# A decoder layer as one software-pipelined program: a straight stream of due times in place of a loop of ticks

## The chip, the cores and the metric

The kernel runs on one core of one Trainium2 chip. The metric is device time in microseconds, the median of several executions. Before the change it is 1157.1 us (three runs, 1156.52 to 1158.71). Line numbers (L896) are those of the kernel before.

## The reference, cut to what matters

Two sequences of 1024 tokens, 256 wide, go through three blocks in fp32, each followed by a residual and a layer norm:

```
x = LN(x + mamba(x))          # rmsnorm, in_proj to 2*512, causal conv of 4 taps, silu, x_proj to (16+16+16),
                              # delta = softplus(dt_proj), scan s = s*exp(delta*A) + delta*B*u over 16 states,
                              # y = sum_n C_n s_n + D*u, y * silu(z), out_proj, + x
x = LN(x + cross_attn(x))     # 8 heads of 32, rope on queries and keys, two sets of 64 keys with one softmax,
                              # out_proj, + x, LN, one expert's linear layer, relu
x = LN(x + moe(x))            # 8 gated experts of 256 and a shared one, top 2 of 8 by softmax, all computed densely
```

Only expert 3 of the cross attention is used. All nine experts of the last block are computed for every token, the weights being zero for those not chosen.

## The kernel before, in words

The 2048 tokens are four chunks of 512 (NT = 4 tiles of 128 rows). Chunks 0 and 1 are one sequence, 2 and 3 the other. The work on a chunk has a *mixer* part (first block) and a *second* part (attention and experts), and the program overlaps the scan of chunk i with the second part of chunk i-1.

One written-out order, SCHEDULE, is walked by each of the five engines (SP issues DMAs); each engine picks the steps in which it has work, and its queue runs them strictly in that order. Semaphores order the engines among each other. `streams` runs the order once for chunk 0 alone, three times in a hardware loop (Fori), and once for the last chunk's second part alone ("drain").

A pass begins with the *pre* steps of chunk i and the last *post* steps of chunk i-1, no scan running: transposes of x, the input projection (L857), convolution (L1140), Silu, the x projection (L829), transposes to C (ctok), the rank product (L836), softplus, delta * u = v on DVE, and for the chunk before the output product (L851), residual and first norm. Then come 35 ticks. In a tick DVE does two scan units (L1105; a unit is one state and 128 channels, 512 steps) and sums two finished state tiles into yacc (L1155); ACT makes the two decays exp(delta*A) in PSUM (L674); POOL multiplies v by the broadcast row of B (L563); PE transposes state tiles (L778). Between these steps, "early", "mid", "half" and "late" carry the second part of the previous chunk by its own tick number.

In the second part, tiles of the attention take two ticks each: score (L896), maximum (L1257), soft maximum on ACT (L729, L733), transpose (L945), copy (L740), value product (L952), scale, small transpose, copy, output projection (L960, L961), sum and statistics. The rope of the queries is made by an ACT copy, a DMA that swaps neighbouring rows, two POOL multiplies and two POOL additions (L583, L587). Then norm, feed-forward (L977, L978), relu, norm, transposes split in a high and a low part, gate logits, top two, weights. The experts are 18 half steps c (nine experts, two halves): first product a (L928), Identity and Tanh on ACT (L766, L768), weighing by the router on POOL (L596), gate product on DVE (L1196), second input product b (L928), hidden product on DVE (L1266) and the second expert product w2 (L908), which adds into two PSUM banks. One half step is done per tick. In PE's queue the order is a(c), w2(c-1), b(c), with the state transposes between.

The two decay buffers are PSUM banks 0 and 1, the state transposes use 2 and 3, the second part 4 to 7; in the drain the first banks serve the experts too. All DMAs are issued from SP's queue in order.

Of the kernel before, what the change touches and what calls it, by code (L numbers as in the profile page):

```python
# [41 lines left out]
HRING = 3  # L43
PREP = 2
DRING = 3
EPS = 1e-5
LINEAR = 30.0
# [13 lines left out]
T_X1T, T_Q, T_ROT, T_S, T_PT = 0, 1, 2, 3, 4  # L61
T_RES = T_PT + 2 * (NT - 1) + 4
T_LNT, T_FFN, T_X2, T_X2T, T_GATE, T_TOP = range(T_RES + 1, T_RES + 7)
T_EXP = T_TOP
T_OUT = T_EXP + 2 * ALL + 1
PRE_TICKS = 2
SCAN_TICKS = 2 * NS + 3


def schedule():  # L70

    tick = lambda t: [("early", t), ("mid", t), ("half", t), ("late", t)]
    steps = [("setup", 0), ("pre", 1), ("post", 3), ("post", 4), ("pre", 2), ("post", 5), ("pre", 3)] + tick(0)
    steps += [("pre", 4), ("pre", 5), ("early", 1), ("pre", 6), ("late", 1), ("setup", 1)]
    for t in range(2, PRE_TICKS):
        steps += tick(t)
    for s in range(SCAN_TICKS):  # L80
        t = PRE_TICKS + s
        steps += [("early", t), ("sum", s), ("mid", t), ("scan", s), ("half", t), ("scan2", s), ("late", t)]
        if 2 <= s < 2 + 2 * ALL + PREP:
            steps.append(("prep", s - 2))
        if SCAN_TICKS - 12 <= s < SCAN_TICKS - 8:
            steps.append(("fetch", s - SCAN_TICKS + 12))
    steps.append(("prep", 2 * ALL + PREP))
    for k, t in enumerate(range(PRE_TICKS + SCAN_TICKS, T_OUT + 1)):
        steps += [("post", k)] if k < 3 else []
        steps += tick(t)  # L90
    return steps


SCHEDULE = schedule()


class Signal:
# [7 lines left out]
    def at(self, j, k):  # L105
        return self.sem, j * self.per + k + 1


def bank_a(c, drain):

    return 0 if drain and c % 2 else 4


def bank_b(c, drain):

    return 1 if drain and c % 2 else 5


def is_first(j):

    return isinstance(j, int) and j == 0


def block_kernel(nc, x, w_in, w_out, w_xp, w_dt, w_q, w_k, w_ks, w_v, w_o, w_f, w_gate, w13, w2, b2, vecs, rows,
                 ctx_t, rope_q, rope_k, out):
    ctx = ExitStack()
    with ctx:
# [15 lines left out]
        wdt = sb("wdt", [RANK, DI])  # L143
# [5 lines left out]
        b2s = sb("b2s", [ALL, DM])  # L149
        vec = sb("vec", [P, VECS])  # L150
        row = sb("row", [1, 2, DM])
        kblk = sb("kblk", [P, SEQS, HB * 2 * KEYS])
        vx = sb("vx", [P, SEQS, HEADS * (HD + 1)])
        ident = sb("ident", [P, P])
        ones = sb("ones", [1, P])
        iota_i = sb("iota_i", [P, EXPERTS], I32)
        iota8 = sb("iota8", [P, EXPERTS])
        keep = sb("keep", [P, CHUNKS])
        power = sb("power", [P, NT])
        neg_a = sb("neg_a", [P, Q * NS])  # L160
# [4 lines left out]
        xt = sb("xt", [P, NT, DM])  # L165
        xn = sb("xn", [P, NT, DM])
        u = sb("u", [P, Q, TC])
        sz = sb("sz", [P, Q, TC])
        delta = sb("delta", [P, Q, TC])
# [3 lines left out]
        hs = sb("hs", [P, 2, Q, TC + 4])  # L173
# [3 lines left out]
        ctok = sb("ctok", [P, NT, NS])  # L177
# [6 lines left out]
        xi = hs[:, 1, :, :]  # L184
        xnt = yacc[:, NT // 2:NT, :]


        x1 = sb("x1", [P, NT, DM])
        x1t = sb("x1t", [P, KD, TC])
        work = sb("work", [P, 4096 + 1024])  # L190
        qr = work[:, 0:2048].rearrange("p (b t) -> p b t", b=HB)
        qs = work[:, 2048:4096].rearrange("p (b t) -> p b t", b=HB)
        qc = [work[:, 4096:5120].rearrange("p (b t) -> p b t", b=2), x1t]
        prob = work[:, 3072:4096]
        probt = work[:, 4096:5120]
        ga = work[:, 1024:2048].rearrange("p (a t) -> p a t", a=2)
        gac = work[:, 2048:3072].rearrange("p (a t) -> p a t", a=2)
        gm = work[:, 3072:4096].rearrange("p (a t) -> p a t", a=2)
        hh = work[:, 4096:5120].rearrange("p (a t) -> p a t", a=2)
# [4 lines left out]
        on = sb("on", [P, DM])  # L204
        ont = sb("ont", [P, KD, P])
# [1193 lines left out]
```

## Time and profile before

| what | value |
|---|---|
| median of three runs | 1157.1 us |
| the profiled execution, whole | 1156.59 us |
| its span, first to last instruction | 1154.8 us |
| mean granted TensorE clock | 0.825 of full |
| busy in the span: PE, DVE, ACT, POOL | 898.6, 793.7, 501.0, 469.3 us |
| first to last scan of chunk 0 | 62.6 to 177.2 us |

The page gives the busy time by engine, a strip in 40 slices, the DMA queues and the chain of work that ended last. The chain is the view to read for this kernel: it goes back from the last instruction to what released it, and so shows which engine's work is in the way and where. Idle time of an engine that is not in the chain costs nothing by itself. The rows used are in the section below.

### The profile page before, as it was taken

Reading aid. Unit: us, or ns where it says so; the run is one execution under the profiler, and the core shown is the slowest. Engines: PE = TensorE matmul, PEld = TensorE weight load, DVE = VectorE, ACT = ScalarE, POOL = GpSimd, SP = SyncE. Lnnn points to the kernel's source line nnn. Section 1 sums busy time; section 2 is a strip of 40 time slices with the busy share of each in tenths; the row PEclk is TensorE's granted clock in tenths of the full one; section 3 lists DMA queues with packets and bytes.
Section 4 is the critical chain, followed back from the end, with each engine's and each line's share of the span. In section 5 each row is a group of like instructions: output and inputs, shape, how many; then the busy total and the mean of one; then the engine's idle time right before and its main releaser. Section 6 shows DMA issues by size and latency. Waiting matters only on the chain.

```text
span 1154.8 us, 13667 instructions
## 1 busy us (share of the span) xinstructions
PE 898.6 (78%) x3960; PEld 681.7 (59%) x3960; DVE 793.7 (69%) x1239; ACT 501.0 (43%) x957; POOL 469.3 (41%) x281
## 2 busy tenths in 40 slices
PE   4934558947879998857789999577799975867995
PEld 2433446446658885356568875265588862645884
DVE  1699996568898957569989864599989751213333
ACT  3545451745434624645535516465445322312232
POOL 1259970074445731273627510654537413000222
PEclk9955557869679999779789999697789996756998
DMA  6136611110205431102025411112045412001451
GB/s 205 47 103 237 234 37 26 67 37 26 103 28 178 152 110 57 74 22 107 19 74 184 154 56 67 64 37 92 19 147 167 153 37 109 1 0 37 155 182 55
DMA packets 43439, 105.65 MB, mean 91 GB/s; under 512 B 4447, under 2 KB 13288, under 8 KB 43358
## 3 DMA queue, kind: packets, MB, share of 16 engines
q1 hardware_dynamic: 43358, 104.68, 26.6%
q8 instruction: 37, 0.61, 0.2%
q14 instruction: 44, 0.36, 0.1%
HBM read 88.73 MB, written 11.74 MB: 87 GB/s over the span
## 4 chain that ended last, share of the span: by engine, by line
PE 61%; DVE 12%; issue 10%; POOL 9%; ACT 5%; DVEq 0%; POOLq 0%; ACTq 0%
PE ps L928 17%; PE ps L908 11%; PE ps L778 9%; PE ps L857 5%; PE ps L896 4%; POOL dbu L563 4%; DVE hs L1105 4%; PE ps L851 2%; PE ps L952 2%; POOL parts L551 2%; PE ps L977 2%; PE ps L836 2%; POOL work L583 2%; DVE yacc L1155 1%; PE ps L960 1%
## 5 line engine op out<-in xcount | busy, mean ns | idle before, releaser
L563 POOL TENSOR_TENSOR dbu<-v,bbc 128x1024 f32<-128x1024 f32 x128 | 301.8, 2368 | 202.5 <-DVE v L1090 117.6
L1105 DVE TENSOR_TENSOR_SCAN hs<-ps,carry,dbu 128x512 f32<-128x512 f32 x256 | 317.1, 1269 | 2.6 <-issue 1.4
L674 ACT ACTIVATE ps<-delta,neg_a 128x512 f32<-128x512 f32 x256 | 176.2, 692 | 231.7 <-DVE hs L1105 231.5
L778 PE MATMUL ps<-ident,hs 128*128 128x128 f32 x1024 | 183.3, 337 | 98.4 <-DVE yacc L1155 83.5
L778 PEld LDWEIGHTS ps<-ident,hs 128*128 128x128 f32 x1024 | 154.8, 177 | 126.6 <-DVE hs L1105 76.8
L928 PE MATMUL ps<-x_hi,parts 128*128 128x512 f32 x576 | 181.4, 438 | 0.0
L596 POOL TENSOR_TENSOR work<-work,cbc 128x512 f32<-128x512 f32 x64 | 82.1, 1283 | 228.4 <-ACT work L766 228.4
L1155 DVE SCALAR_TENSOR_TENSOR yacc<-ps,ctok,yacc 128x512 f32<-128x512 f32 x240 | 167.3, 738 | 1.2 <-PE ps L778 1.0
L908 PE MATMUL ps<-w2s,work 128*128 128x256 f32 x576 | 136.8, 380 | 3.6 <-DVE work L1266 3.6
L908 PEld LDWEIGHTS ps<-w2s,work 128*128 128x128 f32 x576 | 108.2, 189 | 23.1 <-DVE work L1266 5.3
L928 PEld LDWEIGHTS ps<-x_hi,parts 128*128 128x128 f32 x576 | 109.7, 199 | 19.0 <-DVE work L1196 0.6
L766 ACT ACTIVATE work<-ps,half_b 128x512 f32<-128x512 f32 x72 | 49.5, 687 | 153.4 <-PE ps L928 153.4
L1196 DVE SCALAR_TENSOR_TENSOR work<-ps,work 128x512 f32<-128x512 f32 x72 | 49.7, 691 | 88.2 <-POOL work L596 82.1
L896 PE MATMUL ps<-kblk,work 128*128 (+1 forms) x128 | 47.6, 537 | 61.2 <-POOL work L587 47.4
L928 PE MATMUL ps<-x_lo,parts 128*128 128x512 f32 x288 | 92.6, 403 | 0.0
L896 PEld LDWEIGHTS ps<-kblk,work 128*128 128x128 f32 x128 | 33.6, 275 | 72.6 <-issue 55.8
L1266 DVE SCALAR_TENSOR_TENSOR work<-ps,vec,work 128x512 f32<-128x512 f32 x72 | 53.2, 739 | 27.4 <-PE ps L928 21.0
L928 PEld LDWEIGHTS ps<-x_lo,parts 128*128 128x128 f32 x288 | 56.1, 195 | 13.4
L1257 DVE TENSOR_REDUCE mx<-ps 128x8 f32<-128x1024 f32 x16 | 19.5, 1217 | 62.8 <-PE ps L896 62.8
L857 PE MATMUL ps<-yacc,win 128*128 128x512 f32 x128 | 58.3, 616 | 0.8 <-ACT yacc L630 0.8
L768 ACT ACTIVATE ps<-ps,half_b 128x512 f32<-128x512 f32 x72 | 47.0, 653 | 0.0
L569 POOL TENSOR_TENSOR rstd_x<-ve_x,power 128x4 f32<-128x4 f32 x8 | 8.1, 1008 | 93.3 <-DVE ve_x L1176 93.3
(165 smaller groups left out, 1093.6 us busy)
## 6 DMA issues: line engine op xcount, KB each, us to landing
parts<-parts_dram SPq DMA_DIRECT2D x72, 512.0 KB, 3.6
bbc<-brow_dram SPq DMA_DIRECT2D x32, 512.0 KB, 4.5
parts_dram<-parts SPq DMA_DIRECT2D x18, 512.0 KB, 4.0
w2s<-in_w SPq DMA_DIRECT2D x36, 256.0 KB, 4.0
cbc<-comb_dram SPq DMA_DIRECT2D x32, 256.0 KB, 3.6
w13s<-in_w SPq DMA_DIRECT2D x18, 256.0 KB, 3.1
work<-work SPq DMA_DIRECT2D x16, 256.0 KB, 2.3
xn<-in_x SPq DMA_DIRECT2D x5, 512.0 KB, 5.3
```

The lines of the kernel that those rows point to most:

```text
L563: pool.tensor_tensor(dbu[:, i % DRING, :, :], v[:, 2 * h:2 * h + 2, :], bbc[:, n // 2 % 2, n % 2, :].rearrange("p (o t) -> p o t", o=1) .t ...
L596: pool.tensor_tensor(gac[:, ib, :], ga[:, ib, :], cbc[:, g % CRING, :], ALU.mult).then_inc(gac_done.sem, 1)
L674: act.activation(ps[:, unit % 2, :], delta[:, q, :], ACT.Exp, scale=neg_a[:, q * NS + m:q * NS + m + 1]).then_inc(da_done.sem, 1)
L778: last = pe.transpose(ps[:, bank, t * P:(t + 1) * P], src(t), ident[:, :])
L857: last = pe.matmul(ps[:, m % Q, :], win[:, k, m * P:(m + 1) * P], xnt[:, k, :], start=(k == 0), stop=(k == KD - 1))
L896: last = pe.matmul(ps[:, 4 + b // 2, b % 2 * 2 * KEYS:(b % 2 + 1) * 2 * KEYS], qr[:, b, tile * P:(tile + 1) * P], kblk[:, bass.ds(j // CPS ...
L908: last = pe.matmul(out_cols(tile), hh[:, ib, tile * P:(tile + 1) * P], w2s[:, e % WRING, ib * DM:(ib + 1) * DM], start=False, stop=(c == 2 ...
L928: last = pe.matmul(o, left(l, k).bitcast(F32R), right(r, k).bitcast(F32R), start=(i == 0 and k == 0), stop=(i == len(terms) - 1 and k == K ...
L1105: dve.tensor_tensor_scan(hs[:, m % 2, q, 0:TC], ps[:, unit % 2, :], dbu[:, n % DRING, q % 2, :], carry[:, m, q:q + 1], ALU.mult, ALU.add). ...
L1155: dve.scalar_tensor_tensor(out=yacc[:, t, :], in0=ps[:, 2 + t % 2, :], scalar=c, in1=yacc[:, t, :], op0=ALU.mult, op1=ALU.add).then_inc(y_ ...
L1196: dve.scalar_tensor_tensor(out=gm[:, ib, :], in0=ps[:, bank_a(c, drain), :], scalar=1.0, in1=(gac if c >= 2 else ga)[:, ib, :], op0=ALU.ad ...
L1266: dve.scalar_tensor_tensor(out=hh[:, ib, :], in0=ps[:, bank_b(c, drain), :], scalar=col("b3", c), in1=gm[:, ib, :], op0=ALU.add, op1=ALU.m ...
```

## The change

The loop, SCHEDULE and the tick numbers go. Instead there are tables of due times within a period of 32 ticks, sorted by time; `period(j)` merges three chunks: the scan of chunk j, the second part of j-1 (BEFORE, TILE, EXPERT) and the pre steps of j+1 (AHEAD). All five passes are written out. There is no pre stage between scans: the projection, convolution and softplus of the next chunk are among the ticks of the present one. In a tick, PE's state transposes are due at 0.37, and scan units 2n and 2n+1 follow each other on DVE, as do the two decays on ACT, at 0.4. Attention tiles are one tick apart, experts 0.95; steps whose due time is past 32 stand after the last scan of their period. For the last chunk's second part (the fifth period) there is no scan.

```diff
+OWN = {"gates_in_0": 2.7, "gates_raw_0": 3.2, "gates_in_1": 4.5, "gates_raw_1": 5.0, "gates_silu": 14.7}
+BEFORE = {
+    "y_turn": 2.05, "y_skip_1": 2.65, "y_skip_0": 2.95, "y_gate_0": 3.45, "y_gate_1": 3.65,
+    "out_0": 3.7, "out_1": 4.1, "residual_0": 4.35, "residual_1": 4.66, "stats_x1": 4.95, "rstd_x1": 5.05,
+    "norm_x1": 5.4, "x1_turn": 5.7, "x1_keep": 5.9, "query_0": 6.1, "query_1": 6.3, "rope_0": 6.65, "rope_1": 6.95,
+    "stats_xl": 12.65, "rstd_xl": 12.66, "norm_xl": 12.7, "xl_turn": 12.8, "xl_keep": 12.9,
+    "ffn": 13.0, "relu_0": 13.45, "relu_1": 13.65, "stats_x2": 13.7, "rstd_x2": 13.8, "norm_x2": 14.0,
+    "x2_turn": 14.2, "x2_high": 14.4, "x2_low": 14.65, "w2_load": 14.66, "logits": 14.8, "top_two": 15.3, "score_exp": 15.35,
+    "combine": 15.65, "comb_turn": 15.7, "comb_keep": 15.8, "comb_store": 15.82, "out_bias": 16.8,
+    "experts_load": 12.5, "rope_load": 1.7, "x1_load": 0.5,
+}
+TILE = {"score": 7.2, "maximum": 7.65, "soft": 7.7, "p_turn": 8.0, "p_keep": 8.1, "over": 8.15, "over_scale": 8.65,
+        "o_turn": 8.72, "o_keep": 8.76, "o_proj": 9.17, "attended": 9.6}
+TILE_STEP = 1.0
+GATE0, GATE_STEP = 15.8, 0.95
+EXPERT = {"a": 0.0, "gate": 0.01, "w2": 0.1, "b": 0.12, "weigh": 0.13, "product": 0.6, "hidden": 0.95}
+AHEAD = {
+    "x_load": 0.0, "squares": 1.5, "mean_sq": 1.9, "rms": 1.95, "x_scale": 3.0, "x_turn": 5.3, "x_keep": 5.6,
+    "edge": 10.0, "in_0": 11.8, "in_keep_0": 12.3, "conv_0": 12.95, "in_1": 13.4, "in_keep_1": 13.6, "conv_1": 14.1,
+    "edge_keep": 14.12, "conv_silu": 14.71, "xproj": 15.0, "rows_keep": 15.1, "rows_store": 15.11, "c_turn": 15.2,
+    "c_keep": 15.34, "dt_0": 15.4, "soft_in_0": 15.45, "dt_1": 15.75, "soft_in_1": 15.85, "dt_2": 16.1,
+    "soft_in_2": 16.15, "dt_3": 16.3, "soft_in_3": 16.35, "soft_exp": 16.7, "soft_ln": 16.9, "delta": 17.3,
+    "v_0": 28.5, "v_1": 29.5,
+}
+SETUP = {"setup_load": 0.01, "setup_zero": 0.02, "setup_work": 8.5, "setup_keys": 9.5}
...
+        found += [(s + at, name, s, j) for s in range(TICKS) for at, name in ((0.0, "sum"), (0.38, "rows"), (0.4, "scan"))]
...
+        for c in range(2 * ALL + 1):
+            for name, at in EXPERT.items():
+                k = c - 1 if name == "w2" else c
+                if 0 <= k < 2 * ALL:
+                    found.append((GATE0 + GATE_STEP * c + at, name, k, j - 1))
...
+    return [step[1:] for step in sorted(found, key=lambda step: step[0])]
```

Other edits that the steps below touch. The scores sum two products, of the queries times cosine with the keys and of the queries times swapped sine with keys whose neighbouring rows are swapped; the swap is made once per sequence by DMA, and the rope of the queries is two DVE passes per block:

```diff
+                    for b in range(HB):
+                        for s, side in enumerate((qc, qs)):
+                            last = pe.matmul(ps[:, 4 + b // 2, b % 2 * 2 * KEYS:(b % 2 + 1) * 2 * KEYS],
+                                             side[:, b, n * P:(n + 1) * P], kblk[:, s, b * 2 * KEYS:(b + 1) * 2 * KEYS],
+                                             start=(s == 0), stop=(s == 1))
```

Softplus is written as Relu(p) + Ln(1 + Exp(-|p|)), with Abs and Relu on ACT for each of the four channel blocks, Exp and Ln on two blocks at a time, and the sum on POOL; v = delta * u goes from DVE to POOL. The gate half z is copied out raw and put through Silu later, next to the convolution's Silu:

```diff
+                if name == "gates_silu":
+                    act.wait_ge(*zraw_done.at(j, Q))
+                    for h in range(2):
+                        z = sz[:, 2 * h:2 * h + 2, :]
+                        act.activation(z, z, ACT.Silu).then_inc(sz_done.sem, 1)
+                if name == "conv_silu":
+                    for h in range(2):
+                        act.wait_ge(*conv_done.at(j, (TAPS - 1) * 2 * (h + 1)))
+                        c = us[j % 2][:, 2 * h:2 * h + 2, :]
+                        act.activation(c, c, ACT.Silu).then_inc(u_done.sem, 1)
+                    act.preload_act_table(ACT.Exp)
...
+                if name == "delta":
+                    for h in range(2):
+                        pool.wait_ge(*above_done.at(j, Q))
+                        pool.wait_ge(*ln_done.at(j, h + 1))
+                        d = deltas[j % 2][:, 2 * h:2 * h + 2, :]
+                        pool.tensor_tensor(d, above[:, 2 * h:2 * h + 2, :], d, ALU.add).then_inc(delta_done.sem, 1)
```

u, delta and ctok are double; x1 is loaded with x and the residual is made in place; x2 shares its tile with xa; some weight rings share a tile with the convolution's input. The key and value setup on PE and DVE moves from before the first scan to tick 8.5 of the first period.

## Rows read from the trace of the kernel before

**Rows 1.** The page's first part: busy us, share, instructions by engine.
```profile
PE 898.6 (78%) x3960; PEld 681.7 (59%) x3960; DVE 793.7 (69%) x1239; ACT 501.0 (43%) x957; POOL 469.3 (41%) x281
```
**Rows 2.** The chain of waits in order of time, whole span: start, us, what.
```profile
242.85 3.67 PE ps L896 x8
...
497.75 3.79 PE ps L896 x8
...
619.18 1.73 PE ps L908 x8
624.55 1.73 PE ps L908 x8
...
689.66 1.86 issue
...
746.33 3.79 PE ps L896 x8
...
974.01 3.80 PE ps L896 x8
```
**Rows 3.** The chain of waits from 555 to 600 us.
```profile
555.61 1.98 ACT xa L685 x4
...
588.34 0.20 DVE comb L1318
```
**Rows 4.** Timeline of PE, 450 to 522 us: start, us, line, operation, tiles, count.
```profile
450.49 13.90 PE L857 MATMUL ps<-yacc,win 128*128 128x512 f32 x32
...
513.72 1.09 PE L945 MATMUL ps<-ident,work 128*128 128x128 f32 x8 [0.28 <-ACT work L733]
514.65 0.38 PE L778 MATMUL ps<-ident,on 128*128 128x128 f32 x2
516.88 1.97 PE L896 MATMUL ps<-kblk,work 128*128 x8 [1.85 <-ACT ont L745]
...
519.56 1.03 PE L960 MATMUL ps<-wo,ont 128*128 128x256 f32 x4
520.52 0.69 PE L961 MATMUL ps<-row,ones 1*128 1x256 f32 x2
521.14 1.97 PE L952 MATMUL ps<-vx,work 128*128 x16
```
**Rows 5.** The page's fifth part, costliest groups: busy and mean ns, idle before.
```profile
L563 POOL TENSOR_TENSOR dbu<-v,bbc 128x1024 f32<-128x1024 f32 x128 | 301.8, 2368 | 202.5 <-DVE v L1090 117.6
```
**Rows 6.** Timeline of DVE, 53 to 619 us.
```profile
53.66 2.15 DVE L1029 SCALAR_TENSOR_TENSOR work<-ps,vec,work 128x128 f32<-128x128 f32 x8
...
455.50 7.38 DVE L1140 SCALAR_TENSOR_TENSOR u<-hs,vec,u 128x512 f32<-128x512 f32 x11 [0.96 <-ACT u L692]
...
519.20 1.20 DVE L1257 TENSOR_REDUCE mx<-ps 128x8 f32<-128x1024 f32 x1
...
615.93 0.69 DVE L1196 SCALAR_TENSOR_TENSOR work<-ps,work 128x512 f32<-128x512 f32 x1 [0.26 <-POOL work L596]
616.53 1.27 DVE L1105 TENSOR_TENSOR_SCAN hs<-ps,carry,dbu 128x512 f32<-128x512 f32 x1
617.73 0.72 DVE L1266 SCALAR_TENSOR_TENSOR work<-ps,vec,work 128x512 f32<-128x512 f32 x1
```
**Rows 7.** The DMA issues: size and median us from issue to landing.
```profile
xn<-in_x SPq DMA_DIRECT2D x5, 512.0 KB, 5.3
```
**Rows 8.** Timeline of ACT, 477 to 523 us.
```profile
477.30 1.28 ACT L667 ACT_TABLE_LOAD   x1
478.59 2.19 ACT L667 ACTIVATE delta<-delta 128x512 f32<-128x512 f32 x4
...
516.64 1.01 ACT L740 ACTIVATE work<-ps 128x1024 f32<-128x1024 f32 x1
...
520.68 2.18 ACT L733 ACTIVATE work<-ps,top 128x128 f32<-128x128 f32 x8
```
**Rows 9.** Instructions on tile hs, 60 to 182 us: duration min/median/max ns, first and last start.
```profile
L1105 DVE TENSOR_TENSOR_SCAN hs<-ps,carry,dbu x64: 1256/1259/1283, 62.6 to 177.2; 128x512 f32<-128x512 f32 x64
```

More of the change, by code:

```diff
@@ L57 @@
 VECS = _at
[L61 to L91, printed above, removed]
@@ L369, in block_kernel, with streams, bank_a, bank_b @@
         block = ctx.enter_context(nc.Block())
-        def streams(eng, mixer, second):
-            def body(i, first, last):
-                for kind, step in SCHEDULE:
-                    if kind in ("early", "mid", "half", "late"):
-                        if not first:
-                            second(i - 1, step, kind, last)
-                    elif kind == "post" and step >= 3:
-                        if not first:
-                            mixer(i - 1, kind, step)
-                    elif kind in ("setup", "prep"):
-                        if first:
-                            mixer(i, kind, step)
-                    elif kind == "fetch" and not last:
-                        mixer(i + 1, kind, step)
-                    elif not last:
-                        mixer(i, kind, step)
-            for step in range(4):
-                mixer(0, "fetch", step)
-            body(0, True, False)
-            with eng.Fori(1, CHUNKS, 1) as i:
-                body(i, False, False)
-            body(CHUNKS, False, True)
+        def streams(step):
+            for name, at in sorted(AHEAD.items(), key=lambda item: item[1]):
+                step(0, *numbered(name), False)
+            for j in range(CHUNKS + 1):
+                for name, n, chunk in period(j):
+                    step(chunk, name, n, j == CHUNKS)
+        def bank_a(c, drain):
+            return 0 if drain and c % 2 else 4
+        def bank_b(c, drain):
+            return 1 if drain and c % 2 else 5
+        def out_cols(tile):
+            return ps[:, 6 + tile // 2, tile % 2 * DM:(tile % 2 + 1) * DM]
         @block.sync
@@ L848, in mixer @@
+                if name == "out":
+                    for t in (2 * n, 2 * n + 1):
                         for q in range(Q):
@@ new lines, in step @@
+                if name == "over":
+                    pe.wait_ge(*pt_done.at(j, n + 1))
+                    for h in range(HEADS):
+                        c = slice(h * (HD + 1), (h + 1) * (HD + 1))
+                        last = pe.matmul(ps[:, 6, c], probt[:, h * P:(h + 1) * P], vx[:, j // CPS, c],
+                                         start=True, stop=True)
+                    last.then_inc(av_ps.sem, 1)
+                if name == "o_turn":
+                    pe.wait_ge(*on_done.at(j, n + 1))
+                    pe.wait_ge(*p_done.at(j, min(n + 2, NT)))
+                    transposes(5, lambda k: on[:, k * P:(k + 1) * P], KD, ont_ps)
```

1336 lines of the change are left out of this document (666 added, 670 removed).

## The prediction

> **What bounds the kernel now.** I read the busy line first: PE is busy 898.6 us of 1154.8 and DVE 793.7 [rows 1]; neither is full, so the end is set by waits. The chain of waits in order of time says which. The first score product of each of the four chunks' second layers starts at 242.85, 497.75, 746.33 and 974.01 [rows 2], so a chunk costs 254.9, 248.6 and 227.7 us, and from the last of these marks to the end are 180.8. The chain runs through the second layer of the previous chunk (scores, soft maximum, feed-forward, experts); the scan of the current chunk only rides along.
>
> I cut the 248.6 us between the second and third mark into four pieces. (a) Score to the start of the attention's layer norm at 555.61 [rows 3]: 57.9. (b) To the end of the routing weights at 588.54 [rows 3]: 32.9. (c) To the end of the last second expert product at 689.66 [rows 2]: 101.1. In (c) the same expert product recurs at 619.18 and 624.55 [rows 2], every 5.37 us. (d) To the next first score: 56.7, with the skip, gates, output product, both input projections, softplus and rope in it. The test of the change is whether these four pieces shrink.
>
> **The change, part by part.** (1) The loop becomes a straight stream, and the projection, convolution and softplus of the chunk ahead (formerly in d, 45 us with the scan standing still) go between the scan ticks. That frees much of d: half of the input projection (32 issues take 13.90 [rows 4], so a half is 6.9), the x projection (8 issues, 3.5), the rank product (8 issues, 3.5) and the wait for softplus leave it, and the rope no longer goes through a DMA swap and four POOL passes of about the 2.37 us of a POOL multiply over 128x1024 [rows 5]. But the old d began under the last experts; the new one begins only after the final sum. I walk it. Final sums and statistics 3.4. Three pairs of old sums (1.3 each) with two pairs of new scans between (2.4 each [rows 6]): 8.7. DVE's mean of squares stands in this queue and waits for ACT's squares, which come behind its decays (2.4) and behind a load that is queued after the previous output's store and lands in 5.3 [rows 7]: 2 to 6, I take 4. From y's transposes (16 at the pace of 8 in 1.09 [rows 4]) through skip, gate projection, a scan pair and the gate 12. Output product 7. From there through the second half of the gate projection, decays and statistics to the norm 9, transposes and copy 2.7, query product 6.9 (16 issues at the projection's pace), last rope pair 1.4. Together 55.1: (d) is 1.6 shorter.
>
> On the loop's edge PE shows 1.86 us of issue at 689.66 [rows 2], which the straight stream drops; the walk has no such item, so it is already credited. The Trainium skill (Runtime: NRT & Kernel Launch, section "Instruction fetch mechanics") says that a taken branch breaks the sequential prefetch and is a reason to unroll. The row allows at most that for each of three edges, 6 us; a longer stall than this is not in the trace.
>
> (2) Attention: one tile per scan tick instead of one per two, and each score now sums two products (query by keys, swapped query by swapped keys) in place of one. In PE's new order score n+1 stands behind transpose, value product and output projection of the tiles before. So a tile is a ring with no slack: small transpose 0.4, transpose 1.05, copy 1.05, value product 1.95, output projection with its bias row 1.7, score twice 1.8, that is 3.65, maximum 1.2, soft maximum with its bias 2.5: 13.5 us (PE's parts from [rows 4], ACT's from [rows 8], the maximum from [rows 6]). Beside it DVE has one tick (3.7) and 2.7 of tile work, so nothing fills its wait. Piece (a): first score and soft maximum 7.4, three rings 40.5, the last tile 14 (its chain of 4.5, output projection of the tile before 1.7, a state transpose 1, the half input projection that now stands in PE's queue 3.5, its own projection 1.7, residual and copies 1.6), norm statistics 2: 63.9, 6 more than before.
>
> (3) Piece (b): both halves of the convolution (6 taps of 0.67 [rows 6], 4 each) and a Silu block are in it. The block is two table loads of 1.28 [rows 8] and four wide activations of about 1.05 (the 128x1024 copy took 1.01 [rows 8]): 6.8 on ACT. The copy of the x projection is queued behind it, the transpose to C behind that, and DVE's C copy, which stands before the scan and the routing weights, waits for all of them. Norm and copies 4.5, feed-forward 6.7 (four output projections), relu, norm and transposes 10, the second convolution half and a scan 3.5 before the copy to high parts, logits and selection 6, then the wait and the scan 6, weights 2.6: 39.3, 6.4 more.
>
> (4) Piece (c): the Abs and Relu of softplus (8 at 0.65, 5.2), Exp 2.1, Ln and two loads 4.7 are ACT instructions ahead of the third gate, and POOL has the two delta additions (2.37 each [rows 5]) ahead of the third expert's weighing. Three expert steps so take about 21 instead of 16. The other 15: PE needs 5.37 a tick before and after. With the two scans as one block, the hidden product leaves DVE 3.0 after the gate product (two scans of 1.2, 0.65 [rows 6]), when PE has been through a state transpose (1) and the next first half (1.3): PE waits 0.7 in some steps and recovers it in others; I take 5.45, bounds 5.3 and 6.0. The last two steps run after the scan has ended, so they are 2 shorter. (c) is 106.4, 5.3 more. That the second product is one tick nearer in the tables leaves PE's sequence (first half, previous second product, second half) as it was: 0.
>
> The four pieces give 264.7, so a steady chunk is 16 slower. The first gap has no store ahead of the load, 2 less: 262.7, 8 above its 254.9. The third has no chunk ahead: without the half projections, both convolutions, Silu and softplus and with a shorter (d), 231, 3 slower.
>
> (5) Before the first mark. The setup on DVE (53.66 until the first scan at 62.6 [rows 6, 9], 8.9) moves behind the first scans, and half the input projection leaves the start; against it POOL now does two additions, two multiplies and a first product in a row (11.8 [rows 5]) before the second tick. I set the first scan at 58. The 64 scans spread over 62.6 to 177.2 [rows 9], 116 us with the last; into these come the convolution 8, setup 9, and waits: the squares 2.5, PE's setup 3, Silu block and x projection about 9 and softplus about 6, of which some cover each other: I take 15, bounds 0 and 25. That puts the end of this scan at 206 and the first mark at 257, 14 later.
>
> (6) After the last mark: three rings at 13.5 in place of 10 (the score at 516.88 and the value product at 521.14 show the full clock; at 974.01 a score took 3.80 instead of 1.97, the low level [rows 2, 4]); bounds 0 and +30, I take +14, since PE has more to do per ring and its clock rose in the drain's loop before.
>
> Sum against the profiled execution: 1154.8 + 14 + 8 + 16 + 3 + 14 = 1209.8, and 1.8 around the span (1156.59 for that execution, within 0.05% of the median 1157.1): **1212**.
>
> The Trainium skill (ScalarE: Activation LUTs, section "What ACT_TABLE_LOAD costs") gives a load about 1.28 us and a drain of 1.38 after it. The trace shows the load, and the next activation 0.01 us after it (477.30 and 478.59) [rows 8]; by the page the two blocks, four loads, would add 5.5 a period and the sum would be about 1228. I follow the row.
>
> **Rivals.** *Full overlap (0.14).* If the waits in (a) to (c) are covered because the engines run far ahead, a chunk costs what DVE has to do: 793.7 / 4 = 198 [rows 1], with the serial tail 215. First mark as before, 242.9 + 215 + 215 + 195 + 181 + 2 = 1051. For it: DVE idles in both pre stages today. Against: the ring in (2) has one owner of each step, and a queue in order can't pass it. It decides at a ring of about 10 us or less. *ACT blocks hidden (0.14).* The ring is as I say, but decays and gates slip past Silu and softplus: 11 less in two chunks, 5 in the third, 15 at the start, so 1170; the copies before them leave some slack. *All offsets (0.06).* The four pieces and the start end as long as they were: 1157. *Low clock in the rings (0.05).* PE waits in each ring, and its parts (8.75) nearly double: 7.6 more in 9 rings, 1280. The 3.80 us score speaks for it, the 1.97 against.
>
> **Numbers.** The forecast, 1180 to 1245 by itself, has 0.61. The range 1148 to 1255 takes in the hidden blocks and the even case, and leaves out full overlap and the low clock, 0.19. About 0.2% is what this measurement can tell from no change. Faster: 0.14 and a third of the even case, 0.16; same 0.03; slower 0.81.
>
> **What would show it.** Right: successive scores 13 to 14 us apart in the attention stage, DVE idle there on PE; DVE's C copy waiting on ACT after a Silu block; the third gate product late, behind softplus; expert steps of 5.4 to 5.5. The first score of the second layer at about 257, 520, 785. Wrong: score spacing at 10 or less, or scan ticks that go on at 5 us through the attention; then the period is near 215 and the kernel is much faster.

## The result, and the profile after

The changed kernel takes 1388.95 us (median of 4 runs, 1383.93 to 1391.93), 1.200 times the kernel before (95% interval 1.196 to 1.204; 1156.81 in the same job). I had forecast 1212, slower by 55, and a range that ended at 1255. The direction was right; the loss is 232 us, four times what I gave it.

The page's first and second part for the kernel after, which answer to [rows 1] (busy us, share, instructions; then the granted TensorE clock in 40 slices, 9 being nine tenths of full speed or more):

```profile
PE 1031.0 (74%) x4088; PEld 754.9 (54%) x4088; DVE 782.2 (56%) x1202; ACT 507.6 (37%) x915; POOL 476.5 (34%) x275
...
PEclk9577655776667999876668999876569998655898
```

The clock line of the kernel before, for comparison:

```profile
PEclk9955557869679999779789999697789996756998
```

PE's busy time grew by 132 us for 3% more instructions, while the other engines moved by under 12. The doubled scores are some 29 us of that (16 tiles at 1.83, the forecast's price at the full level); for the rest, the same kind of product takes longer. The clock line tells why. Its mean is 0.775 against 0.825 before, and the 5s and 6s come back once in each chunk.

The chain of waits of the kernel after, in order of time (start, us, what), the four marks that answer to [rows 2]:

```profile
293.97 3.73 PE ps L929 x16
...
604.51 3.73 PE ps L929 x16
...
911.68 3.73 PE ps L929 x16
...
1176.00 3.73 PE ps L929 x16
```

The span ends at 1388.0. By these marks the time went as follows; the last column is the run with three remedies together, told below (times of the profiled execution).

| stretch | before | forecast | after | e12_sum |
|---|---|---|---|---|
| to the first score | 242.9 | 257 | 294.0 | 281.2 |
| first to second | 254.9 | 262.7 | 310.5 | 276.5 |
| second to third | 248.6 | 264.7 | 307.2 | 275.8 |
| third to fourth | 227.7 | 231 | 264.3 | 231.3 |
| fourth to the end | 180.8 | 194 | 212.0 | 183.4 |

Here is one attention tile of the kernel after (timeline of PE, ACT and DVE, a selection; in brackets how long the engine stood idle before, and what ended that):

```profile
611.99 1.39 PE L939 MATMUL ps<-ident,work 128*128 128x128 f32 x8 [2.89 <-ACT work L740]
...
614.50 3.62 PE L946 MATMUL ps<-vx,work 128*128 128x33 f32 x16 [1.11 <-ACT work L747]
...
617.93 6.14 PE L929 MATMUL ps<-kblk,work 128*128 128x256 f32 x16
...
624.11 1.23 DVE L1202 TENSOR_REDUCE mx<-ps 128x8 f32<-128x1024 f32 x1 [5.28 <-PE ps L929]
...
625.61 2.18 ACT L740 ACTIVATE work<-ps,top 128x128 f32<-128x128 f32 x8
...
627.93 0.41 PE L794 MATMUL ps<-ident,rows_t 128*128 128x128 f32 x2 [2.98 <-ACT work L740]
...
637.00 0.42 DVE L1224 TENSOR_TENSOR xa<-ps,x 128x256 f32<-128x256 f32 x1 [7.98 <-PE ps L959]
```

The reader is to see two things. The ring is the one that I had walked: score, maximum, soft maximum, transpose, value product, and DVE idle on PE in each link. But the value product takes 3.62 where [rows 4] had 1.97, and the score 6.14 where the first one of a chunk takes 3.72. The same stretch in four windows of one microsecond (the window, its length, PE's busy us and count, granted clock, DMA share, GB/s):

```profile
611.00:612.00 1.00, 0.01 (x1) 1.00 0.00 0
613.00:614.00 1.00, 0.39 (x2) 0.50 0.00 0
621.00:622.00 1.00, 1.00 (x4) 0.50 0.00 0
624.00:625.00 1.00, 0.94 (x9) 1.00 0.00 0
```

PE stands idle for 2.9 us on the soft maximum, works less than 1 us at the full level, and then the granted clock is 0.50 (1.2 GHz) until about 622.7; it comes back for the end of the score and the state transposes, and the next wait begins. So from the second score of a chunk on, scores stand 18.3 to 20.1 us apart where I had 13.5; from the first to the second, where no output projection stands between, 13.4 to 14.0.

Two more places. The first convolution half of the next chunk now runs between scan ticks, beside POOL's products (DVE's timeline for chunks 1 and 2, counted from 0, and the combine weights; then POOL's timeline at the same times):

```profile
128.54 9.20 DVE L1053 SCALAR_TENSOR_TENSOR u<-shared,vec,u 128x512 f32<-128x512 f32 x5 [0.30 <-ACT u L651]
...
375.18 6.15 DVE L1053 SCALAR_TENSOR_TENSOR u<-shared,vec,u 128x512 f32<-128x512 f32 x6
...
426.80 2.14 DVE L1311 TENSOR_TENSOR pr<-el,re 128x32 f32<-128x32 f32 x1
```

```profile
127.66 1.71 POOL L567 TENSOR_TENSOR parts<-xa,parts 128x512 fp32r<-128x512 f32 x1
129.33 2.79 POOL L543 TENSOR_TENSOR dbu<-v,bbc 128x1024 f32<-128x1024 f32 x1
...
426.55 2.35 POOL L543 TENSOR_TENSOR dbu<-v,bbc 128x1024 f32<-128x1024 f32 x1 [14.11 <-DVE hs L1164]
```

A tap takes 1.84 us there (five in 9.20) where [rows 6] had eleven in 7.38, 0.67 each. POOL's product takes 2.79 instead of 2.35 beside them, and a product of 32 columns takes 2.14 and ends when POOL's does. Both taps' operands are in SBUF; the sums and scans, with one operand in PSUM, keep their 0.70 and 1.23 beside the same POOL products.

And the expert step after, with its scan block (ACT, POOL and DVE):

```profile
480.09 0.69 ACT L614 ACTIVATE ps<-delta,neg_a 128x512 f32<-128x512 f32 x1 [0.48 <-DVE hs L1164]
...
480.72 0.67 ACT L782 ACTIVATE work<-ps,half_b 128x512 f32<-128x512 f32 x1
...
481.47 1.27 POOL L595 TENSOR_TENSOR work<-work,shared 128x512 f32<-128x512 f32 x1 [2.21 <-ACT work L782]
...
482.84 0.69 DVE L1258 SCALAR_TENSOR_TENSOR work<-ps,work 128x512 f32<-128x512 f32 x1 [0.82 <-issue]
...
483.44 2.45 DVE L1164 TENSOR_TENSOR_SCAN hs<-ps,carry,dbu 128x512 f32<-128x512 f32 x2
...
485.93 0.69 ACT L614 ACTIVATE ps<-delta,neg_a 128x512 f32<-128x512 f32 x1 [0.48 <-DVE hs L1164]
...
486.56 0.67 ACT L782 ACTIVATE work<-ps,half_b 128x512 f32<-128x512 f32 x1
```

This is a ring that my walk of (c) did not have: gate product, both scans, the decay behind the second scan, and only then on ACT the next gate, its weighing on POOL, and the next product, 5.84 us after the last. [rows 2] have 5.37. Later in the stage, where the drift of 0.05 tick a step has put the sums ahead of the hidden product, steps are 6.0.

### The profile page after: what moved, and what is told of

It reads as the page before. It is cut to its first block, busy times and chain, and to the rows that moved or that the text cites. A ratio compares the mean times of both kernels' runs of the same rounds, so it can differ in the third digit from the quotient of the medians.

```text
span 1388.0 us, 12836 instructions
## 1 busy us (share of the span) xinstructions
PE 1031.0 (74%) x4088; PEld 754.9 (54%) x4088; DVE 782.2 (56%) x1202; ACT 507.6 (37%) x915; POOL 476.5 (34%) x275
## 4 chain that ended last, share of the span: by engine, by line
PE 43%; issue 16%; DVE 13%; POOL 13%; ACT 9%; DMA 1%; DVEq 0%; POOLq 0%; ACTq 0%; SPq 0%
POOL dbu L543 9%; PE ps L929 6%; PE ps L808 6%; DVE hs L1164 4%; PE ps L946 4%; PE ps L1013 4%; PE ps L794 4%; PE ps L917 3%; PE ps L974 2%; ACT work L740 2%; PE ps L799 2%; PE ps L958 2%; DVE yacc L1148 2%; POOL work L595 2%; PE ps L939 1%
## 5 line engine op out<-in xcount | busy, mean ns | idle before, releaser
L543 POOL TENSOR_TENSOR dbu<-v,bbc 128x1024 f32<-128x1024 f32 x128 | 309.4, 2419 | 276.5 <-DVE hs L1164 275.5
L1164 DVE TENSOR_TENSOR_SCAN hs<-ps,nothing,dbu 128x512 f32<-128x512 f32 x128 | 156.7, 1266 | 31.1 <-POOL dbu L543 27.0
L1164 DVE TENSOR_TENSOR_SCAN hs<-ps,carry,dbu 128x512 f32<-128x512 f32 x128 | 156.7, 1266 | 0.0
L1013 PE MATMUL ps<-shared,work 128*128 128x256 f32 x576 | 143.3, 393 | 15.4 <-DVE work L1266 14.7
L595 POOL TENSOR_TENSOR work<-work,shared 128x512 f32<-128x512 f32 x64 | 81.6, 1275 | 185.4 <-ACT work L782 185.4
L1013 PEld LDWEIGHTS ps<-shared,work 128*128 128x128 f32 x576 | 107.7, 193 | 46.4 <-DVE work L1266 16.6
L808 PEld LDWEIGHTS ps<-x_hi,parts 128*128 128x128 f32 x576 | 110.1, 198 | 30.6 <-issue 10.8
L929 PE MATMUL ps<-kblk,work 128*128 128x256 f32 x256 | 85.4, 506 | 3.4 <-DVE work L1196 3.4
L929 PEld LDWEIGHTS ps<-kblk,work 128*128 128x128 f32 x256 | 66.1, 265 | 23.3 <-issue 5.2
L799 PE MATMUL ps<-xnt,win 128*128 128x512 f32 x128 | 72.0, 717 | 1.9 <-ACT rows_t L752 1.1
L946 PE MATMUL ps<-vx,work 128*128 128x33 f32 x256 | 58.0, 403 | 17.8 <-ACT work L747 17.8
L946 PEld LDWEIGHTS ps<-vx,work 128*128 128x128 f32 x256 | 55.8, 330 | 23.2 <-ACT work L747 23.2
L808 PEld LDWEIGHTS ps<-x_lo,parts 128*128 128x128 f32 x288 | 56.0, 195 | 13.5
```

Source lines behind the costliest of these rows:

```text
L543: pool.tensor_tensor(dbu[:, (j * TICKS + i) % DRING, :, :], v[:, 2 * h:2 * h + 2, :], bbc[:, n // 2 % 2, n % 2, :].rearrange("p (o t) -> p ...
L595: pool.tensor_tensor(gac[:, ib, :], ga[:, ib, :], cbc[:, g % CRING, :], ALU.mult).then_inc(gac_done.sem, 1)
L799: last = pe.matmul(ps[:, bank, :], win[:, k, m * P:(m + 1) * P], xnt[:, k, :], start=(k == 0), stop=(k == KD - 1))
L808: last = pe.matmul(ps[:, bank, :], parts[:, c % HRING, part, (s * KD + k) * P:(s * KD + k + 1) * P].bitcast(F32R), right[:, k, :].bitcast( ...
L929: last = pe.matmul(ps[:, 4 + b // 2, b % 2 * 2 * KEYS:(b % 2 + 1) * 2 * KEYS], side[:, b, n * P:(n + 1) * P], kblk[:, s, b * 2 * KEYS:(b + ...
L946: last = pe.matmul(ps[:, 6, c], probt[:, h * P:(h + 1) * P], vx[:, j // CPS, c], start=True, stop=True)
```

## The experiments

All edits are to the changed kernel. Medians are of 4 runs; the ratios are to the kernel before, which ran on the same chip (1154.65, 1155.40 and 1155.49 in the three jobs). The changed kernel's own ratio is 1.200 (1.196 to 1.204). "Less" in us is against its 1388.95, which comes from the job where the kernel before took 1156.81; differences of 2 us between jobs mean nothing.

**e1_warm: keep PE busy in the tile.** Idle transposes are products whose result nobody reads.

```diff
+WARM_TURN, WARM_OVER = 24, 9
...
 if name == "p_turn":
+    pe.wait_ge(*on_done.at(j, n))
+    for _ in range(WARM_TURN):
+        pe.transpose(ps[:, 6, 0:P], ident[:, :], ident[:, :])
     pe.wait_ge(*p_done.at(j, n + 1))
-    pe.wait_ge(*on_done.at(j, n))
...
 if name == "over":
+    for _ in range(WARM_OVER):
+        pe.transpose(ps[:, 4, 0:P], ident[:, :], ident[:, :])
```

> Changed kernel, plus 24 idle transposes of the identity into a free bank in PE's wait for the soft maximum and 9 in its wait for the copy of the turned probabilities, in each of the 16 tiles. Theory 'clock': each tile of the changed kernel takes 18.3 us, of which about 14 are PE work at the low granted clock (value product 3.62, score 5.2 to 6.1, output projection 3.3), because PE sits idle for 3 us on ACT in each tile; with PE kept busy the clock stays up, the value product falls to about 2.0, the score to about 3.7, the output projection to 1.7, a tile takes 12.5 to 14, and 15 tiles save about 5 each: 1389 falls to 1305 to 1325. Rival 'order': the tile is long because score, transpose, value product and output projection stand in one queue, whatever the clock; the added transposes then change nothing or add up to 0.5 per tile: 1385 to 1400.

1353.86, ratio 1.172 (1.169 to 1.175): 35 less, between the two expectations. The products were at the full level in every tile (value product 1.97, score 3.70), yet from the second score on tiles took 16 to 19. In the queue the small transpose of the attention output (o_turn) stands ahead of p_turn and waits for the same soft maximum, so my 24 transposes (3.9 us) came behind that wait and not into it. A bad placement, and no verdict on the size.

**e5_warm2: the same, in the right place.** A step of its own, due 7.71, ahead of o_turn.

```diff
+TILE["warm"] = 7.71
+WARM_TURN, WARM_OVER = 17, 8
...
+if name == "warm":
+    pe.wait_ge(*on_done.at(j, n))
+    for _ in range(WARM_TURN):
+        pe.transpose(ps[:, 6, 0:P], ident[:, :], ident[:, :])
```

> As e1_warm, with the dummies put where PE really waits. In e1_warm the clock was full in every tile (value product 1.97, score 3.72), but the 24 idle transposes stood behind the small transpose of the attention output, which itself waits for the soft maximum, so that 3.9 us of them came onto the chain in tiles two to four. Here 17 stand ahead of that transpose, 8 ahead of the value product. Theory 'clock': a tile falls from 18.3 to 12.3 to 13.8, 5 us less in 12 rings and 2 to 3 at the ends: 1389 to 1315 to 1330. Rival: the tile is as long as in e1_warm, 16 to 17.7, because the order and not the clock sets it: 1345 to 1360.

1311.05, ratio 1.134 (1.132 to 1.135): 78 less, the expectation of "clock". One tile of it:

```profile
599.65 3.70 PE L931 MATMUL ps<-kblk,work 128*128 128x256 f32 x16
...
604.07 2.02 PE L938 MATMUL ps<-ident 128*128 128x128 f32 x17
...
604.89 2.17 ACT L742 ACTIVATE work<-ps,top 128x128 f32<-128x128 f32 x8
...
607.21 0.41 PE L796 MATMUL ps<-ident,rows_t 128*128 128x128 f32 x2 [1.12 <-ACT work L742]
...
609.61 1.97 PE L954 MATMUL ps<-vx,work 128*128 128x33 f32 x16 [0.24 <-ACT work L749]
...
613.08 3.72 PE L931 MATMUL ps<-kblk,work 128*128 128x256 f32 x16
```

From score to score are 13.43 us; I had predicted 13.5. The order of the ring was right, and the clock at which PE ran it was the error: work that computes nothing gave back a third of the loss. The last chunk is not cured: two of its tiles still took 16.4 and 16.6, at a mean granted clock of 0.82 and 0.77.

**e2_first and e6_first2: another order in the tile.** First PE's queue alone, then DVE's and ACT's too.

```diff
-TILE = {"score": 7.2, "maximum": 7.65, "soft": 7.7, ...
+TILE = {"score": 6.95, "maximum": 7.65, "soft": 7.7, ...   (e2_first)
+TILE = {"score": 6.95, "maximum": 7.3, "soft": 7.35, ...   (e6_first2)
```

> Changed kernel with the score of the next tile put ahead of the transpose and value product of the tile before in PE's queue (due at 6.95 instead of 7.2); nothing else. Theory 'order': score, maximum and soft maximum then run beside transpose, value product and output projection of the tile before, PE waits less, and a tile falls from 18.3 to 10 to 14 us: 4 to 8 less in 12 rings, 1389 to 1295 to 1340. Theory 'clock' alone: PE's work per tile (14 us at the low clock) stays the bound and its wait only moves; the tile stays at 15.5 or more and the time at 1355 or more.

1374.98, ratio 1.191 (1.188 to 1.195): 14 less. DVE's maximum still stood behind the scaling that waits for the value product, so the chain stayed in series (tiles of 14.8 to 18.3).

> Changed kernel with score, maximum and soft maximum of the next tile all moved ahead of the value product of the tile before (due 6.95, 7.3, 7.35); no idle transposes. In e2_first only PE's queue had been changed: VectorE's maximum still stood behind the scaling of the attention output, which waits for the value product, so the chain stayed in series. Theory 'order': with both queues changed, a tile is 3.7 score, 1.0 transpose, 1.1 copy, 2.0 value product, 1.8 output projection, 1.1 state transposes, 0.7 and 0.4 for the small transpose and its copy: 12 to 13.5, PE waits under 2 of it and its clock stays up: 1389 to 1310 to 1335. Rival: PE still waits 3 us for the soft maximum behind the small transpose and the clock falls, a tile of 16 or more: 1365 to 1380.

1311.62, ratio 1.136 (1.134 to 1.139): 77 less. With both queues in the new order the soft maximum runs beside the value product:

```profile
614.57 3.69 PE L929 MATMUL ps<-kblk,work 128*128 128x256 f32 x16 [0.57 <-ACT rows_t L752]
...
618.30 1.23 DVE L1202 TENSOR_REDUCE mx<-ps 128x8 f32<-128x1024 f32 x1 [3.39 <-PE ps L929]
...
620.25 1.97 PE L946 MATMUL ps<-vx,work 128*128 128x33 f32 x16 [1.11 <-ACT work L747]
620.33 2.18 ACT L740 ACTIVATE work<-ps,top 128x128 f32<-128x128 f32 x8
```

A tile takes 11.1 to 11.8 us at best, and 12.4 to 14.5 where the clock was low for a part of it. So the loss in the tile can be had back in two ways, by filling the wait or by taking it away; they reach the same time.

**e7_half: the price of the doubled score.**

```diff
-for s, side in enumerate((qc, qs)):
+for s, side in enumerate((qc,)):
...
-                 start=(s == 0), stop=(s == 1))
+                 start=True, stop=True)
```

> Changed kernel that leaves out the second product of each score (swapped query by swapped keys), so half of the score's work. It prices the doubled score alone. Theory 'clock': the score takes 3 of 5.2 to 6.2 us at the low clock, and the rest of the tile stays low: 2.5 to 3 less in 16 tiles, 1389 to 1340 to 1352. Rival, the price that the prediction gave it (1.83 a score at the full clock): 16 by 1.8, 1355 to 1362.

1367.25, ratio 1.179 (1.174 to 1.185; single runs 1354.94 to 1368.47): about 22 less. Fewer than either theory said. A score falls from 5.1 to 6.4 down to 3.5 to 3.8, but the value product stays at 3.62 and tiles, from the second score on, at 16.6 to 17.7. Doubling the score is a tenth of the loss.

**e9_warm_all: the clock outside the tile.** e5_warm2, with idle transposes ahead of xl_turn (28), x2_turn (18) and logits (28).

```diff
+BEFORE.update(warmxl=12.75, warmx2=14.15, warmlg=14.79)
...                                  (and the steps themselves)
```

> e5_warm2, plus idle transposes ahead of three other waits of PE: 28 before the transposes of the attention norm (PE idle 4.8 us there), 18 before those of the second norm (3.3) and 28 before the routing logits (4.8). Theory 'clock': the feed-forward (13.2 us at the low clock) falls to about 6.8, the logits 3.4 to 2.0, the x projection 6.3 to 3.5, and the half input projections from 5.5 to 3.6 where they follow: 10 to 13 less per chunk on top of e5_warm2, 7 in the drain: 35 to 45 less, 1270 to 1295. Rival: between these products the chain runs through ACT and VectorE and hides them: 0 to 12 less than e5_warm2.

1297.65, ratio 1.119 (1.113 to 1.125): 13 less than e5_warm2, just past the rival's end. The feed-forward of chunk 1 falls to 1.13 and 0.69 a tile, from 2.08 and 1.22 (6.8 in all, as expected); that of chunk 0 is still 2.08 and 1.22 in its last two tiles, that of chunk 2 in three and most of the first, and the x projection stays at 6.1 to 6.7. So the filler did not hold the full level outside the tile, and this run does not price that part whole.

**e3_quiet: POOL holds still beside DVE's SBUF work.**

```diff
+if name == "conv":
+    pool.wait_ge(*conv_done.at(j, (TAPS - 1) * 2 * (n + 1)))
+if name == "y_gate":
+    pool.wait_ge(*yg_done.at(j, 2 * n + 2))
+if name == "combine":
+    pool.wait_ge(*comb_done.at(j, 1))
+if name == "mean_sq":
+    pool.wait_ge(*ms_done.at(j, 1))
```

> Changed kernel in which GpSimd waits until the convolution halves, the gate multiplies, the mean of squares and the combine weights are through on VectorE, so that it runs no product beside them; the work is the same. Theory 'contention': convolution taps took 1.5 us on average in the first period and 0.92 in the next two, against 0.74 alone, because their operands are all in SBUF and GpSimd is multiplying in SBUF; with GpSimd quiet each takes 0.67 to 0.75, y_gate 2.5 instead of 4.6 in the first period, the combine product 0.2 instead of 2.1; about 24 us less DVE time in all, of which 10 to 24 come back: 1365 to 1379. Rival: the product that GpSimd delays is then what the next scan waits for, or the slow taps were covered anyway: 1384 to 1392.

1365.00, ratio 1.182 (1.178 to 1.186): 24 less, by a pure addition of waits. The first convolution half of chunk 2 and the combine product, where POOL now comes after:

```profile
366.73 4.06 DVE L1061 SCALAR_TENSOR_TENSOR u<-shared,vec,u 128x512 f32<-128x512 f32 x6
...
416.72 0.19 DVE L1319 TENSOR_TENSOR pr<-el,re 128x32 f32<-128x32 f32 x1
```

6.15 became 4.06 and 2.14 became 0.19. Over the span the 48 taps fell from 46.2 to 37.1 us, the gate multiplies from 12.1 to 9.9, the combine products from 6.6 to 0.8: 17 of the 24; where the other 7 came from I did not trace. Not all of it is the change's doing: the kernel before took 32.5 for its taps, but 6.4 for its combine products. The Trainium skill (SBUF — State Buffer, section "Who interferes with whom") says that a VectorE instruction with two inputs in SBUF contends with a GpSimd instruction that reads SBUF, and that one with at most one SBUF input does not, outside a mode that uses two ports; the taps at 1.84 and 0.67 and the unchanged sums agree.

**e4_split and e11_phase: undo the scan block.** One scan (and its decay) goes back behind the sums; in e11 an expert step is one tick, so that no drift changes the order.

```diff
-for at, name in ((0.0, "sum"), (0.38, "rows"), (0.4, "scan"))
+for at, name in ((0.0, "sum"), (0.01, "scan_first"), (0.38, "rows"), (0.4, "scan"))
...
-GATE0, GATE_STEP = 15.8, 0.95
+GATE0, GATE_STEP = 15.8, 1.0        (e11_phase alone)
-"product": 0.6, "hidden": 0.95}
+"product": 0.56, "hidden": 0.91}    (e11_phase alone)
```

> Changed kernel with the one block of two scans per tick split again: the first scan, and the decay after it, directly behind the sums of the tick, the second where the block was. Theory 'block': in the expert stage the gate product, the block of two scans (2.45), the second decay (0.69), the gate (0.67) and the weighing (1.28) form a ring of 5.84 us, against 5.37 before the change; with one scan between product and gate the steps return to 5.35 to 5.45, some 8 to 11 us less over three chunks, 1389 to 1372 to 1382. Rival: PE's own work sets 5.8 (its second product, two halves and the state transposes), or the first scan so early delays the hidden product: 1385 to 1395.

1382.86, ratio 1.196 (1.192 to 1.200): 6 less, which overlaps with no change. The trace decides where the time doesn't: the steps fell to 5.36 while the order held, as the ring says, and the later ones rose to 7.2, because sums and first scan had drifted between gate product and hidden product.

> e4_split, with the expert steps at 1.0 scan ticks each instead of 0.95 (and product and hidden product due 0.04 earlier), so that the order gate product, second scan, hidden product, sums, first scan holds in every step. In e4_split the expert steps were 5.35 while that order held and 6.0 to 7.2 once the drift of 0.05 a step had put the sums and the first scan between gate product and hidden product; in the changed kernel they are 5.84 and then 6.0. Theory 'block': with the order held, all steps but the first three take 5.35 to 5.5: about 0.5 in 15 steps of three chunks, 20 to 25 less, 1389 to 1362 to 1370. Rival: the steps past the end of the scan, or another engine, take it back: 1380 to 1390.

1356.91, ratio 1.176 (1.171 to 1.181): 32 less, more than expected. Two steps of it (ACT, DVE):

```profile
465.02 0.69 ACT L783 ACTIVATE work<-ps,half_b 128x512 f32<-128x512 f32 x1 [0.63 <-PE ps L809]
465.54 1.27 DVE L1165 TENSOR_TENSOR_SCAN hs<-ps,carry,dbu 128x512 f32<-128x512 f32 x1
...
467.15 0.69 DVE L1259 SCALAR_TENSOR_TENSOR work<-ps,work 128x512 f32<-128x512 f32 x1 [0.34 <-issue]
...
467.76 1.27 DVE L1165 TENSOR_TENSOR_SCAN hs<-ps,carry,dbu 128x512 f32<-128x512 f32 x1
...
472.52 0.69 DVE L1259 SCALAR_TENSOR_TENSOR work<-ps,work 128x512 f32<-128x512 f32 x1 [0.34 <-issue]
```

Products are 5.37 apart, the pace of [rows 2], and the gate now waits only for PE. The three expert stages gave 18 us, the stretch to the first score 9, the stretches from score to routing weights 6.

**e14_tables: the table loads.**

```diff
-act.activation(c, c, ACT.Silu)
-act.preload_act_table(ACT.Exp)
+act.activation(c, c, ACT.Tanh)       (the gate's Silu likewise)
...
-act.activation(d, d, ACT.Ln, bias=1.0)
+act.activation(d, d, ACT.Exp, bias=1.0)
```

> Changed kernel in which Silu and Ln are replaced by functions of the table that is loaded anyway (Tanh, Exp), so that no period loads a table: four loads of 1.28 us a period go, the activations stay. It prices the loads inside the two blocks that the change put between scan ticks. Theory of the prediction (both blocks stand on the chain, between x projection and the C copy and ahead of the third gate): 4 to 5 less in each of four periods, 1389 to 1369 to 1376; with a drain of 1.38 behind each load, as the Trainium skill has it (ScalarE: Activation LUTs, What ACT_TABLE_LOAD costs), twice that. Rival, the loads hide behind PE and the scans: 1384 to 1392.

1370.60, ratio 1.187 (1.182 to 1.191): 18 less. The kernel after has these loads in the blocks (page's groups: busy us and mean ns, idle before), and three single ones at the ends of the program, of which e14_tables keeps one:

```profile
L671 ACT ACT_TABLE_LOAD x4 | 5.1, 1283 | 0.1
L700 ACT ACT_TABLE_LOAD x4 | 5.1, 1283 | 0.1
L701 ACT ACT_TABLE_LOAD x4 | 5.1, 1283 | 0.1
L663 ACT ACT_TABLE_LOAD x4 | 5.1, 1283 | 0.1
```

18 loads of 1.283 are 23.1 us, and 18.3 came back: most of the loads' time stood on the chain, and no more than the loads' time came back. The Trainium skill (ScalarE: Activation LUTs, "What ACT_TABLE_LOAD costs") gives 1.38 more for each; by that page it would be up to 48, an estimate. The measurement decides.

**e12_sum and e13_sum_first: do the causes add?** e12 is e9_warm_all, e3_quiet and e11_phase in one; e13 takes the order of e6_first2 for its tiles, with idle transposes only in each chunk's first tile.

> e9_warm_all, e3_quiet and e11_phase together. If the three causes (PE's clock, GpSimd beside VectorE's operands in SBUF, order of the scans in the expert steps) are separate and none of them hides behind another, their gains add: 1389 - 91 - 24 - 22 = 1252, expected 1240 to 1265. Rival, they overlap (GpSimd held back makes the scan late in the expert stage, or the convolution is hidden once the tile is short): 1270 to 1290.

1253.55, ratio 1.088 (1.082 to 1.095). The single gains are 91, 24 and 32, together 147; 135 were had, so the three overlap by about 12 and are separate in the main. That 1252 was met so closely is in part luck: it had 22 for the third, which measured 32.

> e12_sum with the order of e6_first2 in the tiles (score, maximum and soft maximum ahead of the value product of the tile before) and idle transposes there in the first tile alone. Theory: in e6_first2 a tile took 11.8 us where the clock was full and 13 to 14.5 where it was not; with the clock up, 11.8 against the 13.45 of e5_warm2 saves 1.6 in 12 tiles: 15 to 20 less than e12_sum, 1225 to 1245. Rival: without the idle transposes in the later tiles the clock falls again, and it is no faster than e12_sum.

1274.11, ratio 1.105 (1.100 to 1.110): the rival was right. Without filler in the later tiles the clock fell again (scores of 5.34 to 5.44 in the later tiles of three chunks; mean clock 0.834 against 0.872), and the shorter order gave it away. No version that I ran beats the kernel before.

## Why the prediction was right in sign and wrong in size

**Right.** The end is set by the second layer's chain, and its pieces did not shrink. Piece (d) took 55.2 between the first two marks (549.3 to 604.51; forecast 53.1, the steady 55.1 less 2) and 51.5 between the next two (860.2 to 911.68; forecast 55.1). The sum is near, but the load that waits stood on the chain in the first gap (4.93 us at 556.73) and not in the second, the other way round from my walk. The first scan began at 59.16 (58). DVE idles on PE in the tile, the C copy waits on the Silu block (5.27 in chunk 2, 11.5 in the first period), and the third gate product is late (457.16, 28 us after the routing weights). The signs that I had named were there, but for the sizes: scores stand 18 to 20 apart from the second on, and most steps are 5.8 to 6.0. Both table blocks are on the chain (e14_tables), so the rival "ACT blocks hidden" falls, and "full overlap" with it.

**Step (2), the tile: 13.5 us.** This step failed. It was built from full-level durations, and the low clock stood apart as a rival with 0.05. [rows 2] showed it: the scores on the chain took 3.67 to 3.80 where [rows 4] had one of 1.97. I had read the slow one as an exception of the drain and the quick one as the rule. The change left PE about 3 us of wait on ACT in each tile, with nothing to do behind it in the queue, and the low level came with it in every tile. The kernel before had it in part: 10 of its 16 scores took 2.9 to 3.8. e5_warm2 shows the size (78) and that the ring was else as I had walked it (13.43). The rival's price was too small as well: I gave 7.6 to each of 9 rings, 68, and nothing for the low level in feed-forward, projections and logits (13 more in e9_warm_all). In the first gap, piece (a) took 83.4 (63.9 forecast), and 65.0 in e5_warm2 and in e12_sum. That this comes so near is partly luck: three rings took 38.4 there where I had 40.5, since the first has no output projection in it (11.5), and the first and last steps took 26.6 where I had 23.4.

**Step (3), the moved convolution, "6 taps of 0.67".** The durations came from a place in the old loop where POOL had nothing to do. Moved between scan ticks the same instructions run beside POOL's products and took up to 1.84. I had moved each instruction with its old price and not asked who else works at its new place. e3_quiet gives back 24 us, 9 of them in the taps and 2 in the gate multiplies; the 6 of the combine product are not of this step, for the kernel before pays them too.

**Step (4), "I take 5.45, bounds 5.3 and 6.0".** Measured 5.84 and then 6.0, at the upper bound. My sum had a slip as well: 5 for the first three steps and 1.2 for the other fifteen, less 2, are 4.2 and not 5.3. I had followed the block's effect on the hidden product, and not on the decays, which ACT must issue ahead of the next gate. e11_phase shows it: 32, of which 18 in the three expert stages.

**Step (5), the waits of the first scan, 15 us.** VectorE's timeline of after gives 31 (2.3 for POOL, 2.4 for the squares, 3.3 and 3.2 for sums, 11.5 at the C copy, 4.0 for a decay, 4.0 for POOL), 14 for the setup with its own waits where I had 9, and 20 for the convolution with its waits where I had 8. With 32 ticks of 3.67 behind the first scan at 59.2 that makes 242, where the next chunk's scan begins (242.12). e12_sum takes back 13 of the 37 by which the first mark was late; the other 24 are argued from these rows and were not tried one by one.

**Step (6), the drain, +14:** 31 measured; 15 with the tiles' wait filled (e5_warm2), 8 with the other waits filled too (e9_warm_all), 3 in e12_sum. Most of it was the clock.

The three remedies take back 135 of the 177 us between forecast and result, some 6 of them (the combine products) of a cost that was there before. What the profiled e12_sum still has over the forecast, 38, lies in the first mark (24) and the first two gaps (14 and 11), less 11 at the end. In the first gap pieces (b) and (c) took 51.8 and 120.2 in the changed kernel; in e12_sum they still take 44.8 and 114.7 for the forecast's 39.3 and 106.4. Rows of e12_sum show where (chain of waits, then two gate products on DVE):

```profile
380.73 6.74 PE ps L880 x8
...
409.12 0.69 DVE L1289 SCALAR_TENSOR_TENSOR work<-ps,work 128x512 f32<-128x512 f32 x1 [5.23 <-ACT ps L795]
...
420.00 0.69 DVE L1289 SCALAR_TENSOR_TENSOR work<-ps,work 128x512 f32<-128x512 f32 x1 [4.19 <-issue]
```

In (b) the x projection takes 6.74 where I had 3.5, and the feed-forward 10.8 where I had 6.7: products at the low level that the filler did not reach. In (c) the first gate product begins 7.3 after the routing weights (2.4 before the change), and the first four span 27.4 us (19.6 before the change), 7.8 more where I had 5: Abs and Relu stand ahead of the second gate and POOL's two delta additions ahead of the third weighing, the mechanism that I had named, under-priced. No run moved these steps, so this part is read from rows and not shown. No run took the loop away alone, either: its first edge shows 2.21 us of issue at 440.45, a little more than the 1.86 that I took for all.

## What to carry to other kernels

When a change lines engines up in a ring, price PE's parts at both levels of the clock and look for a wait of PE in each turn: here a wait of 3 us in each tile cost some 5 us more in the products behind it, and useless products put into the wait were worth having. When an instruction is moved, take its duration from its new neighbours: one with both inputs in SBUF slows beside GpSimd, one with an operand in PSUM does not. And when two scans become one block, follow not only what waits behind the block on its own engine, but what another engine must issue for its end before it can go on.

## What the runs showed of the hardware that I had not expected

- A wait of PE of about 3 us in each tile went with a granted clock of 0.50 for some 10 us or more after it; 17 transposes of 2.0 us in all, put into the wait, left 1.1 us of it, and with 8 more ahead of the value product the granted clock was 1.00 from score to score in the first three chunks. The net gain was 78 us of 1389, by 49.5 us of added PE work.
- A VectorE product over 32 columns (0.19 us alone) took 2.14 us when it began 0.25 us after a GpSimd product, and ended with it. The kernel before has the same in its combine step, unseen by me.
- Behind a table load the next activation starts 0.01 us later, and taking 18 loads away gave 18.3 us, no more than the 23.1 of the loads themselves.
